# x added to the output tiles of three blocks by accumulating DMAs from GpSimd, with one exponential and the projections of the second half placed elsewhere

## The reference

```python
s = attention_over_heads(xn)        # per token: q, k, v of 16 x 32 heads (k, v of 8 groups), softmax of 16 x 16 scores
g = silu(ffn(xn))                   # rmsnorm, then down(silu(gate(nx)) * up(nx)), inner size 1792
x = x + s * g
```

## Time and profile before

| what | us |
|---|---|
| time, median of 3 runs (lowest, highest) | 480.94 (480.83, 482.02) |
| time of the profiled execution | 480.94 |
| its span, first to last instruction | 479.2 |
| TensorE busy in it | 468.6 (98%) |
| VectorE busy | 411.2 (86%) |
| ScalarE busy | 243.8 (51%) |
| GpSimd busy | 121.6 (25%) |
| mean granted TensorE clock, of full | 0.996 |

### The profile page before, as it was taken

How to read it: one execution, slowest core, us unless ns; L and a number is a source line. 1 busy time by engine, 2 the same in 40 slices (tenths; PEclk the granted TensorE clock), 3 DMA queues, 4 the chain that set the end, 5 groups by cost and what they waited for, 6 DMA issues and landing times.

```text
span 479.2 us, 6217 instructions
## 1 busy us (share of the span) xinstructions
PE 468.6 (98%) x2122; PEld 391.2 (82%) x2122; DVE 411.2 (86%) x561; ACT 243.8 (51%) x417; POOL 121.6 (25%) x106
## 2 busy tenths in 40 slices
PE   7999999999999999999799999999999999999997
PEld 6898888888887888888687888888888888888886
DVE  6889778987898898888966898899998888888994
ACT  4785666558688888653212245335335334448102
POOL 5740213216222222133235011111111111126920
PEclk9999999999999999999999999999999999999999
DMA  8606997569689966563247558656556655514772
GB/s 270 246 1 230 355 378 263 222 190 306 212 254 307 420 271 253 178 215 122 89 128 269 218 198 316 255 197 221 219 198 220 219 198 198 197 44 133 261 266 88
DMA packets 44623, 105.70 MB, mean 221 GB/s; under 512 B 20272, under 2 KB 21808, under 8 KB 41264
## 3 DMA queue, kind: packets, MB, share of 16 engines
q1 hardware_dynamic: 44592, 105.31, 61.9%
HBM read 69.90 MB, written 35.40 MB: 220 GB/s over the span
## 4 chain that ended last, share of the span: by engine, by line
PE 85%; DMA 3%; DVE 3%; ACT 2%; SPq 2%; issue 2%; POOL 1%; ACTq 0%; POOLq 0%
PE gu_ps L553 16%; PE gu_ps L555 16%; PE gu_ps L556 16%; PE y_ps L687 7%; PE y_ps L689 7%; PE y_ps L688 7%; PE gu_ps L689 3%; PE gu_ps L688 3%; PE gu_ps L687 3%; PE gu_ps L718 2%; PE gu_ps L715 2%; PE gu_ps L714 2%; DMA raw<-down 2%; SPq L319 1%; DMA norm_kept<-norm_out 1%
## 5 line engine op out<-in xcount | busy, mean ns | idle before, releaser
L553 PE MATMUL gu_ps<-z_hi,w_ops 128*128 128x512 f32 x378 | 147.4, 390 | 0.3 <-ACT u L891 0.3
L555 PE MATMUL gu_ps<-z_lo,w_ops 128*128 128x512 f32 x378 | 147.1, 389 | 0.0
L556 PE MATMUL gu_ps<-z_hi,w_ops 128*128 128x512 f32 x378 | 147.1, 389 | 0.0
L498 POOL TENSOR_TENSOR h_lo<-h,h_hi 128x512 fp32r<-128x512 f32 x28 | 37.2, 1330 | 228.5 <-ACT h_hi L916 228.3
L553 PEld LDWEIGHTS gu_ps<-z_hi,w_ops 128*128 128x128 f32 x378 | 71.0, 188 | 16.2 <-ACT u L891 1.1
L556 PEld LDWEIGHTS gu_ps<-z_hi,w_ops 128*128 128x128 f32 x378 | 71.0, 188 | 14.7
L555 PEld LDWEIGHTS gu_ps<-z_lo,w_ops 128*128 128x128 f32 x378 | 71.0, 188 | 14.6
L687 PE MATMUL y_ps<-wd_ops,h_hi 128*128 128x512 f32 x168 | 66.4, 395 | 3.4 <-POOL h_lo L498 3.4
L689 PE MATMUL y_ps<-wd_ops,h_lo 128*128 128x512 f32 x168 | 66.2, 394 | 0.0
L688 PE MATMUL y_ps<-wd_ops,h_hi 128*128 128x512 f32 x168 | 66.2, 394 | 0.0
L916 ACT ACTIVATE h_hi<-h 128x512 fp32r<-128x512 f32 x28 | 17.7, 630 | 62.3 <-DVE h L1211 62.3
(11 more groups left out here) (139 smaller groups left out, 753.6 us busy)
## 6 DMA issues: line engine op xcount, KB each, us to landing
w_kept<-w_ops SPq DMA_DIRECT2D x13, 1792.0 KB, 6.1
w_ops<-w_kept SPq DMA_DIRECT2D x13, 1792.0 KB, 7.5
wd_ops<-wd_kept SPq DMA_DIRECT2D x35, 512.0 KB, 3.8
raw<-gate_up SPq DMA_DIRECT2D x30, 256.0 KB, 5.0
wd_kept<-wd_ops SPq DMA_DIRECT2D x14, 512.0 KB, 7.7
xz<-x SPq DMA_DIRECT2D x16, 256.0 KB, 5.2
raw<-down SPq DMA_DIRECT2D x14, 256.0 KB, 8.2
w_ops<-wd_kept SPq DMA_DIRECT2D x7, 512.0 KB, 7.5
```

Of the source, the lines that this page charges most:

```text
L498: pool.tensor_tensor(lo, src, hi.bitcast(F32), ALU.subtract).then_inc(h_lo_done, 1)
L553: pe.matmul(acc, w_h, z_hi[:, zi, c, :], start=start and c == 0, stop=False, skip_group_check=True)
L555: pe.matmul(acc, w_h, z_lo[:, zi, c, :], start=False, stop=False, skip_group_check=True)
L556: end = pe.matmul(acc, w_l, z_hi[:, zi, c, :], start=False, stop=c == 1, skip_group_check=True)
```

## The change

It has four parts.

- **The add of x.** For blocks 0 to 2 VectorE's add goes. GpSimd issues for each tile a DMA that adds x from DRAM to the gated tile in SBUF (`add_x`): block 0's four ahead of `h_lo_part(28)`, block 1's one each behind `h_lo_part` 31, 32, 34 and 35, block 2's at the end of its queue. `store` waits for these DMAs. `fin_y` has two buffers in turn, so ACT's `y_out` waits for other things, and only block 3 keeps its load of x and VectorE's add.
- **The exponential of pair 2** goes from behind `h_hi_part(18)` to group 14, where `exps` is now called like in the later groups.
- **Projections 11 to 15** run behind products 15, 17, 19, 21 and 23 (before 14, 15, 16, 18 and 20), and VectorE's shares and `t_add`s in the burst are dealt out anew: nine stretches with (0, 0, 2, 6, 5, 5, 4, 3, 2) steps, 27 as before.
- **`load_spread`** stands behind `keep_w`, `keep_wd` and `load_down` of its group.

```diff
-        fin_x = (raw_tiles[:, J:JJ, :], xz[:, 0:J, :], xz[:, J:JJ, :], raw_tiles[:, J:JJ, :])
-        fin_y = raw_tiles[:, 0:J, :]
+        fin_y = (raw_tiles[:, 0:J, :], raw_tiles[:, J:JJ, :])
+        fin_x = xz[:, 0:J, :]
...
-        QKV_BEHIND = (0, 1, 2, 4, 6)
+        QKV_BEHIND = (1, 3, 5, 7, 9)
...
-        BURST_SHARES = (0, 0, 2, 1, 4, 5, 7, 3, 3, 2)
+        BURST_SHARES = (0, 0, 2, 6, 5, 5, 4, 3, 2)
...
+            def load_fin_x():
+                sp.wait_ge(t_lo_done, 8)
+                sp.dma_start(fin_x, x_blocks[3]).then_inc(fin_x_in, 16)
...
             def store(f, tiles=range(J)):
                 for j in tiles:
                     for n, t in enumerate(parts(f, j)):
-                        sp.wait_ge(fin_done, J * f + j + n + 1)
-                        sp.dma_start(out_tiles[J * f + j, :, t], fin_x[f][:, j, t]).then_inc(fin_stored, 16)
+                        if f == 3:
+                            sp.wait_ge(fin_done, j + n + 1)
+                            src = fin_x[:, j, t]
+                        else:
+                            sp.wait_ge(x_added[j], 16 * (f + 1))
+                            src = fin_y[f % 2][:, j, t]
+                        sp.dma_start(out_tiles[J * f + j, :, t], src).then_inc(fin_stored, 16)
...
-                if 6 <= g < 10:
-                    load_spread((g - 6) // 2, ((0, 1), (2, 3))[g % 2])
                 if g:
                     keep_w(g)
                     keep_wd(g - 1)
                     if g + 1 < NI:
                         load_down(g + 1)
+                if 6 <= g < 10:
+                    load_spread((g - 6) // 2, ((0, 1), (2, 3))[g % 2])
...
             for u in range(NI + 3, 2 * NI):
                 load_wd(u)
-                if u == 2 * NI - 4:
-                    load_fin_x(0)
...
                 if g == NI:
                     store(0)
-                    load_fin_x(3)
                 if g == NI + 2:
-                    load_fin_x(1)
-                    load_fin_x(2)
+                    load_fin_x()
...
+            def add_x(f, tiles=range(J)):
+                for j in tiles:
+                    pool.wait_ge(gated_done, J * f + j + 1)
+                    pool.dma_start(fin_y[f % 2][:, j, :], x_tiles[J * f + j], accum_op=ALU.add).then_inc(x_added[j], 16)
+
             for u in range(NI, ITEMS):
+                if u == 2 * NI:
+                    add_x(0)
                 h_lo_part(u)
+                if u - 2 * NI in FINISH_IN:
+                    add_x(1, (FINISH_IN.index(u - 2 * NI),))
+            add_x(2)
...
             def y_out(f, j):
...
-                if f == 0:
+                if f < 2:
                     act.wait_ge(w_lo_a, a_pieces(NI))
-                    act.wait_ge(w_summed, 4 * NI)
+                    act.wait_ge(w_lo_s, NI)
+                    act.wait_ge(wd_lo_done, NI)
                 else:
-                    act.wait_ge(fin_done, J * (f - 1) + j + 1)
+                    act.wait_ge(fin_stored, 16 * J * (f - 1))
...
-                if u == NI + 4:
-                    exps(exps_in(NI))
...
-                if g > NI:
-                    exps(exps_in(g))
+                exps(exps_in(g))
                 h_hi_part(item_of(1, 0, g - NI))
...
                     dve.tensor_tensor(y3, y3, s, ALU.mult).then_inc(gated_done, 1)
-                    if j == n == 0:
-                        dve.wait_ge(fin_x_in[f], 16)
-                    dve.wait_ge(gated_done, tile + n + 1)
-                    dve.tensor_tensor(fin_x[f][:, j, t], fin_y[:, j, t], fin_x[f][:, j, t], ALU.add)\
-                       .then_inc(fin_done, 1)
+                    if f == 3:
+                        dve.wait_ge(fin_x_in, 16)
+                        dve.wait_ge(gated_done, tile + n + 1)
+                        dve.tensor_tensor(fin_x[:, j, t], fin_y[1][:, j, t], fin_x[:, j, t], ALU.add).then_inc(fin_done, 1)
...
-                if n in (1, 3):
-                    t_add(1, n - 1)
-                    t_add(1, n)
+                if n in (1, 2):
+                    t_add(1, 2 * n - 2)
+                    t_add(1, 2 * n - 1)
```

More of the change, by code:

```diff
@@ L157, in build @@
         wd_late_loaded = [sem(f"wd_late_loaded{i}") for i in range(7)]
-        fin_x_in, fin_stored = [sem(f"fin_x_in{f}") for f in range(4)], sem("fin_stored")
+        fin_x_in, fin_stored = sem("fin_x_in"), sem("fin_stored")
+        x_added = [sem(f"x_added{j}") for j in range(J)]
         m1_done, m2_done, m3_done, m4_done = sem("m1_done"), sem("m2_done"), sem("m3_done"), sem("m4_done")
@@ L382, in load_late_wd @@
                   .then_inc(wd_late_loaded[u - LATE], 16)
-            def load_fin_x(f):
-                if f == 0:
[L387 to L394, removed]
+            def load_fin_x():
+                sp.wait_ge(t_lo_done, 8)
+                sp.dma_start(fin_x, x_blocks[3]).then_inc(fin_x_in, 16)
             def store(f, tiles=range(J)):
@@ L944, in y_out @@
                     acc = gu_ps[:, j, t] if f == 3 and n == 0 else y_ps[:, j, t]
-                    act.activation(fin_y[:, j, t], acc, ACT.Silu).then_inc(y_done, 1)
+                    act.activation(fin_y[f % 2][:, j, t], acc, ACT.Silu).then_inc(y_done, 1)
             load_silu()
@@ L1278, in finish @@
                     dve.wait_ge(y_done, tile + n + 1)
-                    y3 = fin_y[:, j, t].rearrange("p (s r) -> p s r", r=REP)
+                    y3 = fin_y[f % 2][:, j, t].rearrange("p (s r) -> p s r", r=REP)
                     s = attn[:, tile, t.start // REP:t.stop // REP].unsqueeze(2)\
```

## The result

| | before | after |
|---|---|---|
| time, median (lowest to highest), 4 runs each | 481.10 us (480.83 to 482.02) | 475.09 us (474.97 to 475.22) |
| time and span of the profiled execution | 480.94, 479.2 | 475.01, 473.2 |
| product 13 to the first matmul of group 14 | 59.07 | 53.27 |
| last matmul's start to the end of the span | 3.8 | 3.8 |

The ratio is 0.9872, 95% interval [0.9855, 0.9889]. The engine table of the changed kernel, to be set beside the earlier trace rows: TensorE has nearly the same work in a shorter span, VectorE has lost its 12 adds, and GpSimd has 12 instructions more.

What follows compares the result with a forecast made beforehand. TensorE's waits and slow clock bound the kernel: 4.95 + 0.97 - 0.3 + 0.4 = 6.0, less 0.15 for GpSimd's price, is 5.85; 480.94 - 5.85 = 475.1 us, range 474.4 to 477.8.

Steps and rivals of the forecast that it cites:

- What bounds the kernel: Only TensorE's waits and slow clock count; the stretch from product 13 to group 14 was 5.95 us over 53.1.
- The exponential, 4.95: Moving it to group 14 removes the wait before product 19 and the slow clock behind: 3.13 + 0.11 + 1.7.
- The projections, 0.67 + 0.3 - 0.3: Even places remove short waits of 0.67 and 0.3 us between products 13 and 26; 0.3 kept for product 26.
- The adds, 0: Moving 12 adds from VectorE to GpSimd's DMAs gains 0, as TensorE doesn't wait for VectorE in groups 14 to 27.
- signs of being wrong: Accumulating DMAs each landing after over 4 us with SP waiting in store, a new group 16 wait, or a longer end.
- the slow-DMA rival: Accumulating DMAs over 4.2 us each make store(0) delay load_w(16), and delay the end; 489.5 us at 6 each; chance 0.06.
- The slack that I gave: Block 0's adds start at 257 and may take 4.2 us each before load_w(16) lands too late for group 16.
- The spread loads, 0.4: Issuing down for item 9 earlier on SP removes TensorE's pause at 145.92; 0.4 us gained, bounds 0.5 lost to 0.5 gained.
- Overhead outside the span: Time around the profiled span, 1.74 us before; 0.15 us was deducted from the gain for GpSimd's unknown DMA price.
- the slow clock behind a pause: From 236.50 to 241.20, behind the long wait, 4.70 us at 0.64 do the work of 3.0, costing 1.7 us.

Runs made afterwards that it cites:

- The exponential alone: Kernel before with only pair 2's exponential moved from behind h_hi(18) to group 14: 475.90 us, ratio 0.9891.
- plain copies: Changed kernel with GpSimd's twelve DMAs copying x without the addition, s * g left out of the output of blocks 0 to 2: 475.17 us, one run.
- the late adds: Changed kernel with block 0's four accumulating DMAs issued behind h_lo(28) instead of ahead of it: 485.95 us, ratio 1.0112.
- the projections alone: Kernel before with only projections 11 to 15 behind products 15, 17, 19, 21, 23, and the new VectorE shares and t_adds: 483.38 us, ratio 1.0038.
- the exponential put back: Changed kernel with pair 2's exponential back behind h_hi_part(18), all else as changed: 482.98 us, ratio 1.0038.
- the kernel with the wait filled: Kernel before with 13 matmuls of unused result put in front of product 19, where TensorE waits: 479.42 us, ratio 0.9955.
- with 768: Changed kernel with dynamic_dma_scratch_size, the space for descriptors of GpSimd's DMAs, 768 bytes instead of 1024: 474.63 us, one run.

## Why the prediction was right

475.1 was forecast and 475.09 measured. By its steps:

- **What bounds the kernel.** Right: TensorE's pauses and its clock are the whole of it. The burst's floor was 53.1, the forecast 53.4, the measurement 53.27.
- **The exponential, 4.95.** The exponential alone gave 5.20: 4.88 for the wait and the clock, and the pause of 0.3 at 251.5, which went with it.
- **The projections, 0.67 + 0.3 - 0.3.** 0.60 measured, the short wait alone, since the 0.3 at 251.5 had gone with the exponential. What remained at product 26 was 0.1, not 0.3. Its `h_lo` took 1.69 us: VectorE had started at 251.90, before GpSimd at 252.59, and GpSimd ended 1.16 after VectorE's 253.12. That is the turn-taking of the Trainium skill, "SBUF — State Buffer", on the shared port pair, which this trace bears out again; the overlap was shorter than at 258.04 in the earlier trace rows (0.5 us against 1.1). Two other `h_lo` of the burst took 2.18 and 2.20 us (at 232.55 and 245.00) and TensorE did not wait, since a projection stood in between: that is what the even places are for. Timelines of VectorE and of GpSimd:

```profile
251.90 1.22 DVE L1239 TENSOR_TENSOR prod<-qkv 128x1024 f32<-128x1024 f32 x1
...
252.59 1.69 POOL L494 TENSOR_TENSOR h_lo<-h_kept,h_hi 128x512 fp32r<-128x512 f32 x1 [3.16 <-ACT h_hi L922]
```

- **The adds, 0.** Right in the sum and in who waits, wrong in the picture. I had four DMAs served one after another, 2.9 us each, the last landed at 268.6 and 464.1. In the trace each takes GpSimd 0.9 us, three are in flight, each lands after 7.4 us (median), and the last land at 261.50 + 7.0 = 268.5 and 458.12 + 5.1 = 463.2. The end came out right by luck: 4 x 2.9 = 11.6 happens to be about what the overlapping ones took, 11.4 both times. One of the prediction's own signs of being wrong was there: all twelve landed after more than 4 us (the quickest after 4.2), and SP stood in `store` from 261.26 to 268.85. It cost nothing, because they overlap; what counts for SP is the time of four together, and the slow-DMA rival, which took four of 4.2 us as one after another, did not happen. The Trainium skill's 2.6 us (an estimate by "DMA: Bandwidth & Descriptors", the section on the anatomy of one DMA on the GpSimd path) is short of all of them: the quickest took 4.2, plain copies beside other transfers 3.0 to 7.6, median 5.2. The slack that I gave, until about 274, was tested by the late adds: beyond it SP's queue does hand the delay to TensorE, as that rival said.
- **The spread loads, 0.4.** Right in place (the pause is gone), and between 0.26 and 0.5 in size; no time could show it.
- **Overhead outside the span**, kept open for GpSimd's first DMA: 1.8 us after, 1.74 before. Nothing.

Beside the landing of the DMAs one more thing was mis-sized, not in the forecast but in three expectations (the projections alone, the exponential put back, the late adds): the slow clock behind a pause. I took the 1.7 us of one profile as its price. The runs of the kernel before show that it isn't one number. Of the 62 taken beside the experiments, 12 had a mean clock of 0.999 or 1.00 and took 478.5 to 480.4 us (mean 479.5), 39 had 0.996 and took 479.9 to 483.0 (481.2), and 11 had 0.993 and took 481.8 to 483.8 (482.8). So behind the same wait the slow clock seems to cost nothing, about 2, or about 3.5 us; where in those runs it fell isn't recorded, but the kernel with the wait filled, at 479.42, agrees with the first group. The changed kernel has no such pause and its four runs lie within 0.25 us. That the profile before fell in the commonest group is luck for the gain of 6 us, which would have been some 4.4 or 7.7 against the means of the others. The forecast of 475.1 hangs less on it, since the clock's cost stands in the time of that same execution and in the sum taken off it.

## What to carry to other kernels

When the bounding engine stands still once, look first for an instruction in another queue that stands there waiting for a third engine, in front of work that is ready. Here one exponential on ACT, 3.4 us of work, held up two products; moved into a gap it cost nothing, and everything else in the change was worth 0.8 us (6.0 less 5.2). A second part that tightens the schedule (the projections in even places) is a gain of 0.6 with the first and a loss of over 2 without it, so test such parts together. A transfer that nobody waits for may take two to three times what you thought; what has to be checked is what stands behind its consumer in an in-order queue.

## What the hardware showed that was not expected

- The slow clock of the kernel with a 3.1 us pause of TensorE is a matter of the run: mean clock 0.999 or 1.00 in 12 of 62 runs, 0.996 in 39, 0.993 in 11, with 479.5, 481.2 and 482.8 us in the mean. Here the pause cost its length and up to as much again.
- GpSimd's DMAs wait in its queue for room for descriptors: with 1024 bytes the fourth accumulating DMA stood 3.62 us, with 768 the third stood 3.59, plain copies hardly at all (four in a row in 2.15 us). Here nothing stood behind them in GpSimd's queue that was wanted sooner.
- An accumulating DMA of 256 KB from GpSimd landed after 4.2 to 9.3 us in the changed kernel, median 7.4 (5.9 to 6.6 in the profiles of five others with the same room), a plain one after 5.2 (median), where a load of 1 MB of x by SP took 5.8 in the earlier trace rows.
